# Four edits around the hand-over from a selective scan to a mixture of experts, one core of a Trainium2

## What is computed

```python
h = layernorm(x) * (1 + ca) + sa
gate = sigmoid(h @ W2 + b2)
u = sigmoid(causal_conv(h @ W1 + b1))                 # 256 channels
xp = u @ x_proj_w                                     # 64 + 16 (B) + 16 (C)
delta = softplus(xp[..., :64] @ dt_proj_w + dt_proj_b)
# for each of 16 states n, along the 1024 tokens of a batch:
#   s_t = exp(delta_t * A_n) * s_(t-1) + delta_t * B_tn * u_t ;  y_t += C_tn * s_t
x = x + ga * ((y + u * D) * gate @ Wo + bo)
h = layernorm(x) * (1 + cb) + sb
probs = softmax(h @ router)                           # 8 experts, the best 2 are kept
x = x + gb * sum over the 2 kept: prob * (silu(h @ gate_e.T) * (h @ up_e.T)) @ down_e.T
```

## Time and profile before

| | us |
|---|---|
| median of the 3 runs | 754.57 |
| the profiled execution, its own time | 750.72 |
| its span, first to last instruction | 748.4 |
| last segment of the scan stage, first to last scan | 476.4 to 530.4 |
| first tile's rows turned by PE | 541.3 |
| last tile's down ends | 734.7 |

### The profile page before, as it was taken

One profiled execution on the slowest core, in us unless ns is written; L12 is line 12 of the kernel. 1 busy time (PEld: TensorE's weight loads), 2 busy tenths in 40 slices (PEclk: granted clock), 3 DMA queues, 4 the chain that ended last, 5 costly groups with the idle time before them and its releaser, 6 DMA issues.

```text
span 748.4 us, 14748 instructions
## 1 busy us (share of the span) xinstructions
PE 641.6 (86%) x4563; PEld 536.3 (72%) x4563; DVE 550.4 (74%) x1170; ACT 539.0 (72%) x1024; POOL 542.4 (72%) x519
## 2 busy tenths in 40 slices
PE   4878889989888989979988976999687998899995
PEld 3434766867657757757766766889577888799984
DVE  4257598899888898987989987999534574355553
ACT  3269989979969997996997997868226644366540
POOL 3148989988999899999999999978615455444432
PEclk9999999999999999999999997999889999999997
DMA  7030534638445334533454333686011222122544
GB/s 221 7 108 4 164 94 109 165 88 255 122 113 143 108 102 135 155 98 98 106 139 130 96 95 106 165 204 162 20 35 56 59 60 64 56 68 63 150 154 155
DMA packets 65196, 82.93 MB, mean 111 GB/s; under 512 B 6960, under 2 KB 55152, under 8 KB 61024
## 3 DMA queue, kind: packets, MB, share of 16 engines
q1 hardware_dynamic: 59648, 70.78, 34.8%
q0 software_dynamic: 4320, 9.12, 3.6%
q10 hardware_dynamic: 1152, 2.10, 0.7%
HBM read 52.19 MB, written 29.78 MB: 110 GB/s over the span
## 4 chain that ended last, share of the span: by engine, by line
PE 44%; ACT 28%; issue 10%; DVE 9%; POOL 5%; another core or an unknown queue 2%; DMA 2%; SPq 0%; ACTq 0%; DVEq 0%; POOLq 0%
PE psum L575 26%; PE psum L579 17%; ACT S L999 9%; ACT dA L1010 8%; DVE ring L1363 3%; POOL ring L550 3%; POOL S L530 1%; ACT xn L902 1%; ACT L937 1%; ACT soft L930 1%; ACT soft L929 1%; ACT soft L937 1%; ACT L1010 1%; ACT hT L884 1%
## 5 line engine op out<-in xcount | busy, mean ns | idle before, releaser
L550 POOL TENSOR_TENSOR ring<-ring,Cb 128x1024 f32<-128x1024 f32 x128 | 303.0, 2369 | 16.6 <-DVE ring L1363 11.3
L1010 ACT ACTIVATE dA<-delta,A 128x512 f32<-128x512 f32 x256 | 178.4, 715 | 12.5 <-DVE ring L1363 10.4
L579 PEld LDWEIGHTS psum<-ident,S 128*128 128x128 f32 x896 | 105.4, 143 | 113.6 <-issue 78.1
L579 PE MATMUL psum<-ident,S 128*128 128x128 f32 x896 | 139.8, 280 | 45.1 <-issue 24.1
L579 PE MATMUL psum<-ident,ring 128*128 128x128 f32 x1088 | 162.5, 281 | 11.1 <-DMA ring<-results 5.4
L1363 DVE TENSOR_TENSOR_SCAN ring<-dA,psum 128x512 f32<-128x512 f32 x128 | 150.5, 1206 | 11.7 <-PE psum L579 7.8
L1363 DVE TENSOR_TENSOR_SCAN ring<-dA,state,psum 128x512 f32<-128x512 f32 x128 | 158.0, 1266 | 1.4 <-PE psum L579 1.0
L999 ACT ACTIVATE S<-duT,BT 128x256 f32<-128x256 f32 x320 | 139.3, 501 | 27.2 <-DVE duT L1106 22.4
L567 POOL DMA_INDIRECT results<-xn,result_at x71 | 68.7, 967 | 107.7 <-DVE xn L1495 61.7
L579 PEld LDWEIGHTS psum<-ident,ring 128*128 128x128 f32 x1088 | 130.9, 145 | 12.5 <-DMA ring<-results 5.7
L575 PE MATMUL psum<-uT,S 128*128 128x128 f32 x852 | 110.6, 281 | 0.6 <-issue 0.5
(11 more groups left out here) (229 smaller groups left out, 814.0 us busy)
## 6 DMA issues: line engine op xcount, KB each, us to landing
Cb<-c_rows SPq DMA_DIRECT2D x32, 1024.0 KB, 6.1
token_rows<-zeros SPq DMA_DIRECT2D x64, 272.0 KB, 7.0
uT<-token_rows SPq DMA_DIRECT2D x71, 68.0 KB
ring<-results SPq DMA_DIRECT2D x8, 512.0 KB, 3.5
xT<-in_xT SPq DMA_DIRECT2D x4, 512.0 KB, 5.0
out_T<-xT ACTq DMA_DIRECT2D x8, 256.0 KB
stage<-in_xT SPq DMA_DIRECT2D x6, 256.0 KB, 8.5
gateup_w<-in_gate SPq DMA_DIRECT2D x1, 1408.0 KB, 9.9
```

The source lines that it names most:

```text
L550: nc.gpsimd.tensor_tensor(ring[:, k % RING], ring[:, k % RING], Cb[:, group_ % 2, own, :].unsqueeze(1).to_broadcast([P, HALVES, BANK]), AL ...
L579: return nc.tensor.matmul(out, block_in, ident[at, at], is_transpose=True, start=start, stop=True, skip_group_check=True)
L1010: nc.scalar.activation(dA[:, (k * HALVES + a) % DA_SLOTS, :], delta[:, s % 2, a, :], ACT.Exp, scale=A[:, a, n:n + 1]).then_inc(da_ready, 1)
```

## The change

- `scale_in` and `turn_in` lose their own way in the last segment: ACT scales duT (256 wide) as in the other segments, all four chunks, and PE transposes.
- In window 7 POOL's scatters of segment 5 come every second gap from 9 to 23, not every third to 30.
- PE turns the first tile's rows, waits for all scans, and does gate_up of tile 0 ahead of the last three sums; the loop leaves that gate_up out. DVE copies the first rows (`turned(0, 0)`) behind gap 5 of window 8, ahead of gap 6 (the one that waits for the sums).
- All 8 combines stand behind the loop on PE, DVE and ACT, in banks 7 and 6 by turns, each waiting for the half two before it. SP loads halves 0 to 5 at tiles 63 to 68 in a row (before at 63, 64, 66, 67, 69 and 70).

```diff
-MIX_STEPS = (64, 65, 67, 68, 70, 71)
+MIX_LOADS = 63
-        PX, PM = bank(6)[:, 0:P], bank(7)
+        PX = bank(6)[:, 0:P]
         def PMX(h):
-            return bank(6) if h == BATCH * SEG - 1 else PM
+            return bank(7 - h % 2)
-        def tile_schedule(eng, tile, beside, combine, late_):
-            for t in range(TILES + 2 + late_):
+        def tile_schedule(eng, tile, beside, combine):
+            for t in range(TILES + 2):
...
                 tile(t, t - rnd * XS_SLOTS, rnd)
-                if t - late_ in MIX_STEPS:
-                    combine(MIX_STEPS.index(t - late_))
-            for h in range(len(MIX_STEPS), BATCH * SEG):
+            for h in range(SEGS):
                 combine(h)
...
                 load(t)
-                if t == MIX_STEPS[0] - 1:
+                if t == MIX_LOADS:
                     results_given(OLD_TILES)
                     sp.wait_ge(summed, STEPS * HALVES)
-                if t + 1 in MIX_STEPS:
-                    load_results(MIX_STEPS.index(t + 1))
+                if 0 <= t - MIX_LOADS < EARLY_SEGS:
+                    load_results(t - MIX_LOADS)
             results_given(TILES)
-            for h in range(len(MIX_STEPS), SEGS):
+            for h in range(EARLY_SEGS, SEGS):
                 load_results(h)
...
-                if f is not None and 9 <= gap and gap % 3 == 0:
-                    if gap == 9:
-                        scatter_ready(f)
-                    scatter(f, (gap - 9) // 3 // TOPK, (gap - 9) // 3 % TOPK)
+                if f is not None:
+                    i, rest = divmod(gap - 9, 2 if window == SEGS - 1 else 3)
+                    if rest == 0 and 0 <= i < TOPK * CS:
+                        if i == 0:
+                            scatter_ready(f)
+                        scatter(f, i // TOPK, i % TOPK)
...
                 for c in range(CS):
-                    if s < SEGS - 1:
-                        last = turn(db(k, a)[:, c * P:(c + 1) * P], S[:, k % S_SLOTS, c, a * P:(a + 1) * P])
-                    else:
-                        last = product(db(k, a)[:, c * P:(c + 1) * P], duT[:, s % 2, c, a * P:(a + 1) * P],
-                                       S[:, k % S_SLOTS, c, 0:P])
+                    last = turn(db(k, a)[:, c * P:(c + 1) * P], S[:, k % S_SLOTS, c, a * P:(a + 1) * P])
...
-            for k in range(STEPS - LAG, STEPS):
-                for a in range(HALVES):
-                    add_state(k, a)
-            for gap in range(TAIL_GAP):
-                gap_work(gap, SEGS)
...
-                if h == BATCH * SEG - 1:
+                if h == 1:
                     pe.wait_ge(xt_read, TILES)
-                else:
-                    wait(pe, mt_read, h)
+                wait(pe, mt_read, h - 1)
...
-                if k < TILES:
+                if 0 < k < TILES:
                     gate_up(k, par)
...
+            pe.wait_ge(group[0], GROUP_STEPS[0])
             pe.wait_ge(xs_loaded[0], 16)
             turn(PX, xs[:, 0, 0:HID]).then_inc(xt_filled, 1)
-            tile_schedule(pe, tile, beside, combine, 0)
+            pe.wait_ge(loaded["gateup"], 32)
+            pe.wait_ge(scanned, STEPS * HALVES)
+            gate_up(0, 0)
+            for k in range(STEPS - LAG, STEPS):
+                for a in range(HALVES):
+                    add_state(k, a)
+            for gap in range(TAIL_GAP):
+                gap_work(gap, SEGS)
+            tile_schedule(pe, tile, beside, combine)
...
                 for c in range(CS - pool_chunks(k)):
-                    if s < SEGS - 1:
-                        nc.scalar.activation(S[:, k % S_SLOTS, c, :], duT[:, s % 2, c, :], ACT.Identity,
-                                             scale=BT[:, s % 2, c, n:n + 1]).then_inc(scaled_act, 1)
-                    else:
-                        nc.scalar.activation(S[:, k % S_SLOTS, c, 0:P], ident[:, :], ACT.Identity,
-                                             scale=BT[:, s % 2, c, n:n + 1]).then_inc(scaled_act, 1)
+                    nc.scalar.activation(S[:, k % S_SLOTS, c, :], duT[:, s % 2, c, :], ACT.Identity,
+                                         scale=BT[:, s % 2, c, n:n + 1]).then_inc(scaled_act, 1)
...
-            turned(0, 0)
-            tile_schedule(dve, tile, beside, combine, 1)
+            for gap in range(TAIL_GAP):
+                if gap == TAIL_GAP - 1:
+                    turned(0, 0)
+                gap_work(gap, SEGS)
+            tile_schedule(dve, tile, beside, combine)
```

More of the change, by code:

```diff
@@ L720, in turn_in @@
                 wait(pe, scanned, HALVES * k + a - DBU_BANKS + 1)
-                s = k // NSTATE
                 for c in range(CS):
-                    if s < SEGS - 1:
-                        last = turn(db(k, a)[:, c * P:(c + 1) * P], S[:, k % S_SLOTS, c, a * P:(a + 1) * P])
-                    else:
-                        last = product(db(k, a)[:, c * P:(c + 1) * P], duT[:, s % 2, c, a * P:(a + 1) * P],
-                                       S[:, k % S_SLOTS, c, 0:P])
+                    last = turn(db(k, a)[:, c * P:(c + 1) * P], S[:, k % S_SLOTS, c, a * P:(a + 1) * P])
                 last.then_inc(turned_in, 1)
@@ L818, in beside @@
                 gap_work(gap % GAPS, SEGS + gap // GAPS)
-            pe.wait_ge(loaded["gateup"], 32)
-            pe.wait_ge(group[0], GROUP_STEPS[0])
             def gate_up(k, par):
@@ L1074, in combine @@
                 act.dma_start(outT_d[:, cut_], xT[:, cut_]).then_inc(stored, 16)
-            tile_schedule(act, tile, beside, combine, 2)
+            tile_schedule(act, tile, beside, combine)
             act.wait_ge(stored, 16 * BATCH * SEG)
```

## The result

The changed kernel takes **746.16 us** (median of 6 runs, 744.93 to 749.00) against 755.12 for the kernel before beside it (6 runs, 752.45 to 756.65). The ratio is 0.9889, with an interval of [0.9865, 0.9913]: 8.4 us by the ratio, 9.0 by the medians, where 10.6 was forecast. So the two traces differ by only 4.0 us, and the traces alone don't explain the whole gain. Of the later executions, one of the kernel before (1255 us) and one of after_fill (901 us) were in a slow state and are in no ratio.

A forecast was written before the change was run, and what follows sets the result against it. DVE was taken to bound the last segment, a chain of waits the hand-over, and PE the tile loop. Gains of 4.2 at the hand-over and 6.4 from the combines made 10.6: 754.57 - 10.6 = 744.0 us, range 739.5 to 751.0.

The forecast's parts named there:

- the head: From DVE's last scan to its copy of tile 3's turned rows; the gain forecast at this hand-over was 4.2 us.
- Part 1: Last segment's B: ACT's 7.0 us of longer scalings hidden, PE relieved of 14.6 us, gain taken as 0.9 us.
- the router's wait: Last segment: 0.9 of DVE's 1.11 us idle before the router's maximum goes, so routing ends at about 532.9.
- rival of a falling clock: Last segment: PE, with mostly transposes, held at half clock, costs 14 us, giving 758; chance 0.06.
- Part 2: Scatters moved earlier: eighth starts near 524.3, first rows in SBUF at about 529.6; no gain of its own booked.
- before anything can use them: Hand-over: the first rows, in SBUF at about 529.6, would arrive before any work could use them.
- the head gives nothing: Rival at the hand-over: sums slip behind half-clock gate_up, yT0 stays near 545; about 747.5 us, chance 0.14.
- Part 3: Hand-over: gate_up of tile 0 ahead of the last sums brings the second half's turn sooner; gain 4.2 us (1.5 to 7.0).
- Part 4: Combines moved out of the tile loop, halves 0 to 5 hidden behind half 6's load; gain 6.4 us.
- The last tiles: From the copy of tile 63's rows to the last row scaling's end; 5.3 us were to leave the loop.
- the tail: From the end of the last row scaling to the span's end; last two combines forecast at full clock, 1.9 us.
- contention: At the end, six stores meet two loads: between 0 and 1.5 us of delay, taken as 1.0.

The follow-up runs named there:

- after_fill: The changed kernel plus idle transposes on PE (6 ahead of the turn of tile 0's rows, 22 behind it) while it waits for DVE's routing: ratio 0.9859.
- no_b: The changed kernel, but in the last segment PE again multiplies duT by a scaled unit matrix: 744.24 us, ratio 0.9896.
- no_order_fill: The changed kernel with the last sums again before tile 0's gate_up, plus 8 idle transposes on PE ahead of each of the last three pairs of sums: ratio 0.9889.
- only_scatters: The kernel before with one edit, the last early segment's eight scatters every second gap: 745.25 us, ratio 0.9904.
- no_order: The changed kernel, but the last sums and their tail again come before tile 0's gate_up: 745.58 us, ratio 0.9887.
- no_combines: The changed kernel, but six combines with their loads and stores are back in the tile loop: 749.36 us, ratio 0.9951.
- only_combines: The kernel before, with only the move of all combines behind the tile loop: 749.69 us, ratio 0.9966.

## Why the prediction was right, and where it was not

The time was right: 744.0 forecast, 746.16 measured, inside 739.5 to 751.0. Two of its four terms were not, and that the sum came so near is in part luck: by the runs of one part alone the head gave 7.2 us where 4.2 was forecast, and for another reason, and the combines 2.6 where 6.4 was forecast. The two errors nearly cancel.

**Part 1 held, with nothing to gain.** ACT's scalings grew as forecast (63 of them of 495 ns in the segment) and were hidden: ACT waited 4.1 us for DVE's scans over the decays, and DVE stayed the bound. PE's busy time fell by 7.1 us, where 14.6 was forecast. The 0.9 us taken from the router's wait did not come: the routing ended at 533.46, not at 532.9, and no_b has the same time. The wait itself did go, for the router's maximum (528.48) now has no idle time before it. But DVE waits at two other places, where before it did not:

```profile
479.37 0.19 DVE L1171 TENSOR_REDUCE stat<-psum 128x4 f32<-128x32 f32 x1 [0.74 <-ACT psum L968]
...
494.85 0.69 DVE L1126 SCALAR_TENSOR_TENSOR yg<-gate,psum 128x512 f32<-128x512 f32 x1 [0.37 <-PE psum L579]
```

In all it waits 1.1 us in the segment after and 1.4 before, and the segment is 0.2 us shorter. The rival of a falling clock came in part, and cost next to nothing: in the change the clock was 0.50 from 492 to 496, and over the segment it was 0.91 to 0.97 in the eight traces with part 1 against 1.00 in the six without. It was 1.00 in the window at 522, in which PE only transposed. The rule that the full clock does not engage for transposes (the Trainium skill, "TensorE: Matmul & The Clock Gate", section "Part 4: PE-mode transpose") is contradicted once more by no_order_fill, whose window at 536 holds only transposes and shows 1.00.

**Part 2 was booked at nothing, and carries the head.** The positions were about right: eighth scatter at 525.58 (forecast 524.3), rows turned at 530.96 (529.6), POOL's last product at 535.87 (534.8; before, 535.69, so it came no sooner). The step that failed is "before anything can use them". I read the wait for rows before, but not what stood behind it on PE: the turn of tile 0 ahead of the prefix products, and so the positions and yT0. Without that wait yT0 moves from 545.04 to 539.43 in the old order too (only_scatters). The rival "the head gives nothing" had the same gap.

**Part 3 did what it said and gained nothing.** gate_up at 534.07 (533.2), sums ending at 540.14 (539.4), yT0 at 542.59 (542.1), the second turn at 544.89 (545.4): each within 0.9 us, with the half clock at the start as chosen. But its 4.2 us were set against the kernel before instead of against part 2 alone. Beside no_order the order saves 1.7 us from the last scan to the second half's turn and has lost it by tile 3, since that turn (1.12 us instead of 0.66) and tile 1's gate_up (2.56 instead of 1.50) run at the half clock. That the clock costs this order some 2.7 us is shown by after_fill in the trace, for the head: 18.4, where the five traces with this order as it is have 20.1 to 21.4. In the times the two intervals overlap.

**Part 4 was mis-sized at the end, not in the loop.** The last tiles gave 5.9 us (forecast 5.3 out of the loop and 0.5 at the last down). In the tail 0.6 us of gain were forecast: the last two combines at the full clock, less 1.0 of contention. It lost 4.0 instead: SP issued the loads 0.7 us later behind the last row scaling (0.2 of that is the start of the last scatter, 0.5 its landing, beside the first stores), and the load of half 7 was there 8.20 us after the issue where the last combine before began after 5.00 (its start at 743.23 less the issue at 738.23), 3.2 more. So part 4 is worth 1.9 us in the trace of the change, 2.6 (1.0 to 4.1) by its own run and 4.7 (2.0 to 7.4) by no_combines. The failed step took the bytes of both streams together (6.5 us) and compared them with the time at hand, as if the loads came through first. They share with the stores: half 7 lands nearly last. Of the 3.4 us by which the last packet of the loads came later (7.68 us after the issue instead of 4.25), 1.8 are there when 95% of the packets have ended, and 1.6 come with the last few, behind an instruction packet at 735.0. The slices moved at up to 480 GB/s while both were in flight:

```profile
GB/s 0 0 0 151 0 292 353 311 372 127 377 231 38 66 207 311 348 372 480 353 353 363 419 386 344 47 24 268 344 28 5 0 0 0 0 0 259 344 0 0
```

These are the 17.4 us from 727 in 40 slices. They include 419 and 480, above the 358 GB/s that the Trainium skill names ("DMA: Bandwidth & Descriptors", "Where 436 GB/s comes from"), but also holes of 38, 66, 24 and 47. What makes the holes is open; the two orders of stores that I tried did not shorten the tail.

**What stays open.** In the trace the head and the last tiles, less the tail, give 5.3 us, and the last segment 0.2. The time fell by 8.4. The spans differ by less than these terms, 4.0, because tiles 3 to 63 took 1.7 us longer in the profiled execution of after. The other way, from 5.5 to 8.4, nothing is shown: the profiled execution of before lay 4.4 us below its median, and what its other executions had longer is not in a trace; only_combines, with the same head, has 26.0 there instead of 24.5. By the times part 2 alone (7.2) and part 4 alone (2.6) make 9.8, and both together measured 10.1. That parts 1 and 3 add anything to that is not shown, nor that they cost.

## What to carry to other kernels

When a wait is taken away, look at what is queued behind the waiting instruction on its engine, and price that alone before a second edit is credited: here moving eight scatters carried the head, and the reordering around them gave nothing that the runs can tell. A transfer that the end waits for shares the way with whatever was issued just before it: price it as landing with the last of those bytes, not by its duration alone. And where the clock falls in short waits, one trace of a stretch is one draw: the same instructions took 16.7, 18.4 and 21.5 us.

## What the runs showed that I had not expected

Waits of 1.2 us on PE left the clock at 1.00 in one execution and were followed by its fall in another, with the same instructions in the same order; what decides is not shown here.

The tile loop has stalls that the trace gives to no known releaser. In the chain of waits of the change:

```profile
611.43 5.61 another core or an unknown queue
```

Every one of the 14 traces has one at tile 24, where the next tile's copy comes 2.43 to 2.53 us later than the 2.12 of a tile, each time with a 16 KB packet of the instruction queue nearby; four to seven stalls of over 1.5 us between tiles 24 and 62 add up to between 9.4 us (before) and 15.5 (no_order). They were not tried, and differ between executions by more than some of the parts studied here.
